# The next batch's eighth projections ahead of the output projection in TensorE's order

## The reference

```python
x = x + tanh(g_xattn) * attention(layernorm(x), ctx, ctx)
# in attention:
q = queries @ Wq + bq; k = keys @ Wk + bk; v = values @ Wv + bv   # 16 heads of 64
scores = where(causal, -1e30, where(mask, -1e30, q @ k.T / sqrt(64)))
out = (softmax(scores) @ v) @ Wo + bo
# then, for each expert i
out = out + (relu((x * (argmax(x @ Wr + br) == i)) @ W1[i] + b1[i]) @ W2[i] + b2[i])
x = x + tanh(g_ffn) * out
```

## Time and profile before

| | |
|---|---|
| median of 3 runs | 398.24 us (398.19 to 400.45) |
| profiled execution | 399.0 us |
| its span, first to last instruction | 397.1 us |
| mean granted TensorE clock | 0.962 |
| TensorE busy | 363.3 us |
| VectorE, ScalarE, GpSimd busy | 277.5, 247.6, 193.6 us |

### The profile page before, as it was taken

How to read it: one execution, slowest core, us unless ns; L and a number is a source line. 1 busy time by engine, 2 the same in 40 slices (tenths; PEclk the granted TensorE clock), 3 DMA queues, 4 the chain that set the end, 5 groups by cost and what they waited for, 6 DMA issues and landing times.

```text
span 397.1 us, 11299 instructions
## 1 busy us (share of the span) xinstructions
PE 363.3 (91%) x2829; PEld 292.5 (74%) x2829; DVE 277.5 (70%) x1300; ACT 247.6 (62%) x908; POOL 193.6 (49%) x373
## 2 busy tenths in 40 slices
PE   3969998999999999999999999999999978859991
PEld 1847777777777777777777777777777757759991
DVE  3189993988498859868894989498846654645661
ACT  1767874686587748766874876577735523636661
POOL 7037363456446634663564466446633523253552
PEclk9999999999999999999999999999999975878996
DMA  6897201002000200030002002000000037232320
GB/s 204 202 367 196 85 22 62 3 2 80 33 0 0 83 27 0 0 109 0 0 10 99 0 0 92 30 0 0 3 24 2 2 117 257 94 87 82 85 69 12
DMA packets 20552, 25.21 MB, mean 63 GB/s; under 512 B 3545, under 2 KB 16677, under 8 KB 20528
## 3 DMA queue, kind: packets, MB, share of 16 engines
q1 hardware_dynamic: 18544, 19.40, 16.2%
q0 software_dynamic: 1984, 5.53, 3.9%
HBM read 18.48 MB, written 6.90 MB: 64 GB/s over the span
## 4 chain that ended last, share of the span: by engine, by line
PE 69%; DVE 8%; issue 7%; ACT 7%; DMA 3%; another core or an unknown queue 1%; DVEq 1%; SPq 1%; POOL 1%; ACTq 0%; POOLq 0%
PE ps_kv L1158 13%; PE ps_o L1158 12%; PE ps_s L1158 11%; PE ps_t L1231 9%; PE ps_t L1158 8%; PE ps_w L1158 7%; PE ps_q L1158 6%; ACT prob L557 3%; DVE masked L752 3%; PE ps_s L1436 1%; DMA sorted_rows<-rows,slot_i 1%; DMA bias_rows<-in_L_ffn_b 1%; DVE rank L847 1%; ACT hidden L656 1%
## 5 line engine op out<-in xcount | busy, mean ns | idle before, releaser
L422 POOL TENSOR_SCALAR prob<-prob,row_inv 128x128 f32<-128x128 f32 (+1 forms) x256 | 104.7, 428 | 144.8 <-DVE row_inv L765 144.8
L557 ACT ACTIVATE prob<-masked,neg_max 128x128 f32<-128x128 f32 (+1 forms) x256 | 113.6, 446 | 68.0 <-DVE neg_max L752 68.0
L752 DVE CUSTOM_DVE_ANT_0 masked<-ps_s,mask_now 128x128 f32<-128x128 f32 (+1 forms) x256 | 78.9, 353 | 23.8 <-PE ps_s L1158 19.7
L771 DVE COPY prob_T<-ps_t 128x384 f32<-128x384 f32 x128 | 67.5, 548 | 1.2 <-PE ps_t L1231 1.2
L1158 PE MATMUL ps_s<-k_T,q_T 64*128 64x128 f32 (+1 forms) x512 | 59.3, 350 | 1.9 <-DVE neg_max L752 1.8
L1231 PE MATMUL ps_t<-ident,prob 128*128 128x128 f32 x384 | 56.4, 282 | 1.5 <-DVE prob_T L771 1.3
L1231 PEld LDWEIGHTS ps_t<-ident,prob 128*128 128x128 f32 x384 | 41.1, 141 | 22.6 <-issue 16.8
L1158 PE MATMUL ps_o<-prob_T,v_nat 128*64 128x256 f32 (+1 forms) x512 | 56.0, 340 | 0.0
L557 ACT ACTIVATION_READ_ACCUMULATOR prob<-masked,neg_max 128x1 f32 x256 | 48.3, 189 | 0.0
L1158 PEld LDWEIGHTS ps_o<-prob_T,v_nat 128*64 128x64 f32 x512 | 31.1, 136 | 17.4 <-issue 2.2
L1158 PEld LDWEIGHTS ps_s<-k_T,q_T 64*128 64x128 f32 x512 | 33.6, 186 | 12.3 <-issue 11.1
(11 more groups left out here) (196 smaller groups left out, 577.4 us busy)
## 6 DMA issues: line engine op xcount, KB each, us to landing
ctx_buf<-in_ctx SPq DMA_DIRECT2D x8, 768.0 KB
tile_in<-sorted_rows SPq DMA_DIRECT2D x24, 128.5 KB
sorted_rows<-pad_rows POOLq DMA_DIRECT2D x6, 385.5 KB, 3.7
packs<-in_L_ffn_W SPq DMA_DIRECT2D x1, 2048.0 KB
packs<-in_L_ffn_W SPq DMA_DIRECT2D x8, 256.0 KB
ctx_nat<-in_ctx SPq DMA_DIRECT2D x8, 128.0 KB, 4.0
x_nat<-in_x SPq DMA_DIRECT2D x1, 896.0 KB, 9.2
sorted_rows<-pad_rows SPq DMA_DIRECT2D x2, 385.5 KB
```

The costliest lines, as they stand in the source:

```text
L422: g.tensor_scalar(prob[:, slot, lo:hi], prob[:, slot, lo:hi], row_inv[:, slot, t:t + 1], 1.0, ALU.mult, ALU.mult).then_inc(prob_ready, 1)
L557: s.activation(prob[:, slot, lo:hi], masked[:, slot % 2, lo:hi], ACT.Exp, bias=neg_max[:, slot, t:t + 1], scale=-1.0, accum_out=row_sum[:, ...
L752: v.tensor_tensor_reduce(out=masked[:, slot % 2, lo:hi], in0=ps_s[slot % 2][:, lo:hi], in1=mask_now[:, lo:hi], scale=-SCALE, scalar=FLOOR, ...
L771: v.tensor_copy(prob_T[:, slot % TSLOTS, :], ps_t[slot % 2][:, 0:W3]).then_inc(probT_kept, 1)
```

## The change

At the end of each batch but the last, TensorE now issues q of pair 7 of the next batch, then k and v of it, and then the output projection. Before, the first batch had k and v, the output projection and then q, and the loop had the output projection, q, and then k and v. The waits move with their work, and no other engine's order changes.

```diff
--- before.py
+++ after.py
@@ -1389,14 +1389,10 @@
                         router(b - 1)
                 if last:
                     last_projection(PAIRS - 1)
-                elif first:
+                else:
+                    project_q(b + 1, 7)
                     project_kv(b + 1, 7)
                     output_projection(b)
-                    project_q(b + 1, 7)
-                else:
-                    output_projection(b)
-                    project_q(b + 1, 7)
-                    project_kv(b + 1, 7)
 
             pe.wait_ge(ident_ready, 1)
```

## The result

The changed kernel takes 403.4 us (median of 12 runs) against 398.29 us for the kernel before beside it (12 runs). The ratio is 1.011, 95% interval 1.0072 to 1.0148, that is +4.4 us (2.9 to 5.9). The medians lie 5.1 us apart; the ratio compares the means of the runs and leaves out one slow run of the changed kernel (406.04 us). The profiled execution took 403.79 us with a span of 401.9 us, 4.8 us over that of before.

What follows compares the result with a forecast made beforehand. TensorE was taken to set the pace, busy 363.3 of 397.1 us. Six loop boundaries (+5.0 to +5.6) less 0.8 at the first gave +4.5 us on 398.24, so 402.7 us; range 400.9 to 404.3.

Steps and rivals of the forecast that it cites:

- TensorE ahead of ScalarE, and the free products as cover: At loop boundaries, seven output projection products needing nothing new occupy TensorE while ScalarE catches up; pause before 0.77 us.
- Step 1: Loop boundary: k and v start 0.49 us after v_nat starts; q fits inside that wait and costs nothing more.
- Steps 2 and 3: Loop boundary: k and v take 0.87 us, then the output projection runs in one piece for 3.57, without pausing for o_T.
- Step 4: Loop boundary, last work to next scores: the scores' start costs 0.20 to 0.31 us extra; boundary 0.83 to 0.94 later.
- The first boundary: Batch 0's end: scores 0.33 us earlier as q fits the pause, 0.5 back at the in_T wait; together -0.8 us.
- The sum: Six loop boundaries, +5.0 to +5.6 us, less 0.8 at the first: +4.2 to +4.8, taken as +4.5 us.
- What else moves: At loop boundaries VectorE, ScalarE and GpSimd get work earlier, but VectorE then waits for the scores; costed at nothing.
- A: Loop boundary cheaper: scores' start free or a weight load ready after the wait; +2.5 to +3.6 us; chance 0.16.
- B: Faster: early release of other engines moves ScalarE's late exponentials of turn 7 forward; down to -5.4 us; chance 0.03.
- C: Dearer: no first-boundary gain, or early k_T and v_nat delay something unseen; +5.3 to +6.2 us; chance 0.09.
- The weight loads: At boundary waits no weights are fetched during the wait; otherwise 0.15 us a boundary hidden, sum +3.6 not +4.5.
- Rival D: Loop boundary pause halves TensorE's clock, doubling the 3.57 us output projection: +21 us over six, some 424 us; chance 0.02.

Runs made afterwards that it cites:

- e1: Changed kernel, with ScalarE's q_T, k_T and v_nat copies of pair 6 moved ahead of the last turn's exponentials; ratio 0.9838 to the kernel before.
- e3: Changed kernel, with the output projection cut in two: seven products, then q, k and v, then nine products; ratio 0.9895 to the kernel before.
- e6: Changed kernel, with only ScalarE's q_T copy of pair 6 moved ahead of the last turn's exponentials; ratio 1.0056 to the kernel before.
- e7: Kernel before, with the changed order at the first boundary only and the loop as before; ratio 0.9973 to the kernel before.
- e5: Changed kernel, reordered to k and v, output projection, then q at every boundary; 412.01 us, ratio 1.0457 to the kernel before.
- e8: Order of e5 with the early ScalarE copies of e1; ratio 0.9951 to the kernel before.

## Why the prediction was right

- **TensorE ahead of ScalarE, and the free products as cover**: shown. Taking the lateness away (e1) or giving the cover back (e3) both turn the loss into a gain. The periods came out as worked out (36.32 for 36.3, 36.43 for 36.44); in the runs e3 gained 4.2 us of its 6.2.
- **Step 1, v_nat to k and v**: 0.49 us forecast, 0.48 measured. From q_T to q it was 0.50 from start to start (139.12 to 139.62), where the forecast had 0.58 (138.29 to 138.87). This hides in the second wait either way, and e6 confirms that q costs nothing.
- **Steps 2 and 3**: 0.87 forecast and measured (141.18 - 140.31). The projection to the next scores is 3.78, that is 3.57 and 0.21.
- **Step 4** is where the choice lay, 0.20 to 0.31 for the start of the scores. It is 0.21, and the boundary costs 0.83, the low end of the forecast. The other 0.11 was, as the prediction allowed, q directly ahead of k and v: in e1 k and v start at 135.23 behind q and the projection 0.98 later, not 0.87. Nor is the 0.2 a matter of the loop. In the middle of a batch the step from v's loads to values(7) is 62.41 - 61.66 = 0.75, to the output projection 65.47 - 64.92 = 0.55. The 0.2 stands where loads of 128*128 are followed by 128*64 or 64*128.
- **The first boundary**: -0.93 instead of -0.8, since the 0.11 of step 4 is saved there too, q no longer standing right ahead of the scores (0.44 instead of 0.33; the prediction counted this term in the loop and left it out here), and 0.49 for in_T as forecast.
- **The sum**: +4.05 in the trace, against +4.2 to +4.8 summed and +4.5 taken; the runs say +4.4 (2.9 to 5.9). The trace is 0.15 under the summed range, for step 4 and the first boundary both came out low. That the ratio lies within 0.1 of +4.5 is luck; the evidence is in the period. The time of 403.4 us is 0.7 over the forecast, and single runs of the changed kernel lie between 399.8 and 406.0.
- **What else moves, costed at nothing**: right. VectorE's 4.64 us wait became 1.63 and 4.14 at the scores, and the next turns show the gaps of before.
- **The rivals**: A's mechanism did not happen, neither a free start of the scores (0.21) nor a load made ready during the wait. B did not: ScalarE's q_T starts 1.71 us after the loads of values(7) as before, and its late exponentials still wait 1.48 us for VectorE (1.50 before). C did not: the gain at the first boundary came, in this trace and alone in e7.
- **The weight loads**: the forecast went by the row that nothing is loaded during a wait, and q's load and matmul start together at 139.62 again. The rule of the Trainium skill (TensorE: Matmul & The Clock Gate, Part 2) speaks of matmuls in flight; across a wait on a semaphore no run here shows a load pulled ahead.
- **Rival D, the clock**: did not happen here. With 2.27 us of waiting, in the order of e5, it did, at four boundaries, and cost some 1.6 us each where D had put 3.57: the clock was low over a part of the projection and not all of it.

## What to carry to other kernels

Before moving work ahead of a block that waits late, look at what that block's free part covers. Here seven products that needed nothing new hid an engine's backlog, and the work moved ahead of them asked for that backlog at once. Of the orders tried on TensorE alone, the one that interleaves was best: free part, then the waiting work, then the rest (e3, 1.1% faster than before). Where the late engine has idle time ahead of its own backlog, that engine can be reordered instead (e1, 1.6% faster; its period is the shortest found, 36.32 against 36.43, though the intervals of the two ratios overlap). Both together were not tried. The same edit can have opposite signs at a loop's first boundary and in its body, so each place is costed by itself.

## What was not expected of the hardware

TensorE's granted clock fell behind a wait of 2.27 us in an otherwise busy loop (e5). It did so at four of the five loop boundaries with this wait, with a mean of 0.68 over the projection at two of them and some 1.6 us lost each time. It stayed at 1.00 at the fifth and behind the 2.09 us of the first loop boundary. Waits of 1.58 and 0.39 us with q's product between them (the changed kernel) and of 1.44 us (e6) left it at 1.00. That a clock falls after idleness is what the Trainium skill says (TensorE: Matmul & The Clock Gate, Part 1); that a pause of 2.27 us can be enough, and only at some of like boundaries, these runs show. That the pause is the cause rests on e8 alone, with the reserve on the chip made there.
